# A language model tower on one core: mixer, dense layer and experts as one stage, with one written list of steps per engine

## What is computed

```python
h = layernorm(token_emb[ids] + type_emb[type] + pos_emb) * gamma + beta
h = h + attention(layernorm(h))                  # 8 heads of 192
x = layernorm(h)
z = layernorm(x) * g1 + b1                       # the mixer
q, k, v = split(z @ in_w.T + in_b)               # 12 heads of 16
x = x + (softmax(q @ k.T / 4) @ v) @ out_w.T + out_b
x = x + gelu(x @ mlp_w1 + mlp_b1) @ mlp_w2 + mlp_b2     # the dense layer, 192 -> 768 -> 192
xm = layernorm(x) * g2 + b2
gates = softmax over the 2 largest of xm @ gate_w.T + gate_b
for e in range(4):                               # the experts, each 192 -> 768 -> 192
    x = x + gates[e] * (gelu(xm @ w1[e] + b1[e]) @ w2[e] + b2[e])
return h + x
```

## Time and profile before

| | |
|---|---|
| three runs | 911.65 us median (911.03 to 914.28) |
| the profiled execution | 905.92 us, span from first to last instruction 904.2 us |
| PE, PEld busy | 804.1 us (89%), 721.8 us (80%) |
| DVE, ACT, POOL busy | 532.7 us (59%), 477.0 us (53%), 267.3 us (30%) |
| granted TensorE clock, mean | 0.963 |
| attention | 0 to 423.6 us |
| mixer | 423.6 to 587.4 us |
| dense layer | 594 to 654 us |
| experts | 654 to 904.2 us |

### The profile page before, as it was taken

The page is one execution under the profiler, slowest core; times in us unless marked ns, Lnnn a source line. Parts: engine busy times, 40 slices in busy tenths (PEclk is TensorE's granted clock), DMA queues, the critical chain, the costliest instruction groups (busy, mean ns, idle before and its releaser), DMA issues. The chain is left out here.

```text
span 904.2 us, 16184 instructions
## 1 busy us (share of the span) xinstructions
PE 804.1 (89%) x5880; PEld 721.8 (80%) x5880; DVE 532.7 (59%) x1404; ACT 477.0 (53%) x1282; POOL 267.3 (30%) x479
## 2 busy tenths in 40 slices
PE   0398999999999999986679897779899999999997
PEld 0298999999999999986558676668778898888987
DVE  4855454545555455345687777437877565665564
ACT  2255363635354444441575878555555665566654
POOL 6372020202020202021246779600207024061060
PEclk9999999999999999998786999899999999999999
DMA  8353333333332323331101111030000000000000
GB/s 241 99 107 71 78 73 71 80 70 80 71 80 70 80 70 79 72 80 45 48 1 62 63 62 41 23 93 1 1 1 1 1 18 1 19 1 1 18 1 18
DMA packets 33615, 47.30 MB, mean 52 GB/s; under 512 B 4672, under 2 KB 28608, under 8 KB 33536
## 3 DMA queue, kind: packets, MB, share of 16 engines
q1 hardware_dynamic: 28240, 34.63, 16.0%
q0 software_dynamic: 2544, 9.05, 3.4%
q10 hardware_dynamic: 2752, 2.59, 1.1%
HBM read 30.53 MB, written 15.73 MB: 51 GB/s over the span
## 5 line engine op out<-in xcount | busy, mean ns | idle before, releaser
L1524 DVE TENSOR_TENSOR ffn_hid_lo<-ffn_gelu,ffn_hid_hi 128x512 fp32r<-128x512 f32 x120 | 95.6, 799 | 105.4 <-ACT ffn_hid_hi L1498 104.2
L1452 PE MATMUL ffn_ps_out<-ffn_weights_w,ffn_hid_hi 128*128 128x384 f32 x480 | 144.1, 357 | 3.0 <-DVE ffn_hid_lo L1524 2.6
L1494 ACT ACTIVATE ffn_gelu<-ffn_ring,ffn_b 128x512 f32<-128x512 f32 x120 | 82.3, 686 | 110.8 <-PE ffn_ring L1441 107.1
L454 POOL TENSOR_SCALAR attn_probs<-attn_probs,attn_inverse 128x128 f32<-128x128 f32 x128 | 48.1, 376 | 288.4 <-DVE attn_inverse L744 280.6
L1453 PE MATMUL ffn_ps_out<-ffn_weights_w,ffn_hid_lo 128*128 128x192 f32 x480 | 120.6, 251 | 0.0
L1452 PEld LDWEIGHTS ffn_ps_out<-ffn_weights_w,ffn_hid_hi 128*128 128x128 f32 x480 | 90.0, 188 | 9.9 <-DVE ffn_hid_lo L1524 5.1
L1453 PEld LDWEIGHTS ffn_ps_out<-ffn_weights_w,ffn_hid_lo 128*128 128x128 f32 x480 | 91.3, 190 | 4.1
L937 POOL TENSOR_SCALAR mix_probs<-mix_probs,mix_inverse 128x128 f32<-128x128 f32 x192 | 73.9, 405 | 56.3 <-DVE mix_inverse L1188 56.3
L613 ACT ACTIVATE attn_probs<-ps_scores,attn_neg_max 128x128 f32<-128x128 f32 x128 | 45.4, 366 | 77.6 <-DVE attn_neg_max L740 77.6
L1498 ACT ACTIVATE ffn_hid_hi<-ffn_gelu 128x512 fp32r<-128x512 f32 x120 | 75.9, 632 | 3.8
L1382 POOL TENSOR_SCALAR ffn_bias_part<-ffn_b,ffn_gates 128x192 f32<-128x192 f32 x64 | 37.4, 602 | 134.9 <-DVE ffn_gates L1558 133.8
(11 more groups left out here) (272 smaller groups left out, 2182.8 us busy)
## 6 DMA issues: line engine op xcount, KB each, us to landing
v_rows<-attn_v_flat SPq DMA_DIRECT2D x16, 768.0 KB, 3.3
attn_v_rows<-v_rows SPq DMA_DIRECT2D x128, 96.0 KB, 3.7
mix_stage<-in_w POOLq DMA_DIRECT2D x5, 576.0 KB, 4.9
mix_stage<-in_w POOLq DMA_DIRECT2D x10, 192.0 KB, 3.3
mix_stage<-in_w POOLq DMA_DIRECT2D x5, 384.0 KB, 4.1
attn_stage_main<-in_w_qkv SPq DMA_DIRECT2D x2, 768.0 KB, 8.1
h_rows<-hin SPq DMA_DIRECT2D x8, 192.0 KB, 2.0
ffn_base<-h_rows SPq DMA_DIRECT2D x1, 1536.0 KB, 9.2
```

The lines of the kernel that those rows point to most:

```text
L454: last = nc.gpsimd.tensor_scalar(probs[:, n, j, :], probs[:, n, j, :], inverse[:, n, j:j + 1], float(D) ** -0.5, ALU.mult, ALU.mult)
L1452: nc.tensor.matmul(ps_out[:, b, 0:2 * D], hid_hi[:, i % 3, tile], w2[:, c, :, :], start=c == 0, stop=False)
L1494: nc.scalar.activation(gelu[:, i % 2, :], ring[:, bank("L1", i), :], ACT.Gelu, bias=b1[:, f * HC + c:f * HC + c + 1]).then_inc(chunk_read, 1)
L1524: nc.vector.tensor_tensor(hid_lo[:, i % 3, :], gelu[:, i % 2, :], raw(hid_hi[:, i % 3, :]), ALU.subtract).then_inc(lo_ready, 1)
```

## The change

`mixer` and `experts` become one function, `mixer_and_feed_forward`, one block. The numbers of what is computed stay the same.

- The dense layer is worked in 8 pairs of tiles as soon as a pair's mixer output is there. DX transposes its rows, D1 makes two hidden slices of 256 tokens in one bank (10 matmuls of 256 columns), DE is the gelu of each half on ACT, DG the hi copy, now on POOL, and the lo on DVE, D2 the second layer of one tile into a ring bank, DF the addition on DVE.
- Up to expert chunk 11 the order is no longer one list: `ORDERS` holds a list for each of PE, ACT, DVE and POOL. Behind that the old pattern goes on. Norms of the experts' rows (EN) of units 0 and 1 are in the lists, those of units 2 and 3 among the later chunks.
- Accumulators of the second expert layer are the banks of the mixer's scores, and buffers of the experts reuse memory of the mixer's; added waits guard both (`exps_ready`, `v_ready`, `out_filled`, `d2_filled`).
- Weight loads, expert constants and per-unit loads of h1 are issued from SP's queue, at the block's start for the first layer, instead of POOL's and ACT's. Weights 0 and 1 are split among the mixer's steps, 2 and 3 at the lists' end, 4 behind.

```diff
-def mixer(nc, keep, dram):
+def mixer_and_feed_forward(nc, keep, dram):
...
+    TWO = 2
+    PT = TWO * P
+    DENSES = TILES // TWO
+    BLOCKS = HC // 2
...
+        ORDERS = {
+            "pe": """X:0.0 X:0.1 Q:0.0 Q:0.1 Q:0.2 V:0.0 V:0.1 V:0.2 S:0 V:0.3 S:1 X:1.0 X:1.1 S:2 S:3 T:0 T:1 Q:1.0 S:4 A:0 Q:1.1 O:0 T:2 S:5 S:6 T:3 Q:1.2 A:1 T:4 S:7
...
+            "dve": """N:0.3 X:0.0 X:0.1 N:1.0 N:1.1 N:1.2 Q:0.1 Q:0.2 V:0.0 V:0.1 V:0.2 S:0 V:0.3 S:1 W:0.0 J:0 N:1.3 J:1 S:2 X:1.0 X:1.1 S:3 L:0 J:2 S:4 A:0 L:1 J:3 W:0.1
...
+        for i in range(FIRST, len(chunks)):
+            chunk(i)
...
+        def walk_order(engine, do):
+            for step, i in first_steps[engine]:
+                do[step](i)
+            for step, i in order:
+                if step in do:
+                    do[step](i)
...
+            def dense_his(i):
+                p, k = i
+                pool.wait_ge(d_gelu, BLOCKS * p + k + 1)
+                if p:
+                    pool.wait_ge(d2_filled, TWO * p)
...
+            def dense1(i):
...
+                slot_free("D1", i)
...
+                for c in range(2):
+                    cols, to = slice((2 * k + c) * P, (2 * k + c + 1) * P), slice(c * PT, (c + 1) * PT)
+                    for n, (w, x, part) in enumerate(passes):
+                        last = nc.tensor.matmul(ring[:, bank("D1", i), to], w[:, cols], x[:, part, :], start=n + c == 0, stop=n == 4 and c == 1)
...
+            def dense_gelu(i):
...
+                for c in range(2):
+                    part = slice(c * PT, (c + 1) * PT)
+                    last = nc.scalar.activation(dgelu[:, k, part], ring[:, bank("D1", i), part], ACT.Gelu, bias=b1[:, 2 * k + c:2 * k + c + 1])
```

More of the change, by code:

```diff
@@ L839, in mixer @@
[L839 to L877, removed]
@@ new lines, in mixer_and_feed_forward, with second, chunk @@
+        for part in range(3):
+            put(FIRST + part, ("H", (4, part)))
+            put(FIRST + part + 1, ("W", (4, part)))
+        def second(i):
+            order.append(("L2", i))
+            if i % HC == HC - 1:
+                order.append(("EF", i // HC))
+        def chunk(i):
+            early = i % HC == LAG - 1 and i >= LAG
+            if early:
+                second(i - LAG)
+            order.append(("L1", i))
+            if i >= LAG and not early:
+                second(i - LAG)
+            order.extend(after.get(i, ()))
@@ new lines, in steps_of @@
+        def steps_of(engine):
+            for word in ORDERS[engine].split():
+                kind, _, place = word.partition(":")
+                numbers = tuple(int(n) for n in place.split("."))
+                yield kind, numbers if len(numbers) > 1 else numbers[0]
+        first_steps = {engine: list(steps_of(engine)) for engine in ORDERS}
+        order = []
+        for i in range(FIRST, len(chunks)):
+            chunk(i)
+        for i in range(len(chunks) - LAG, len(chunks)):
+            second(i)
@@ L1045, in project_out, with turn_rows @@
                 last.then_inc(out_filled, 1)
-            walk_order({"X": transposes, "Q": project_qk, "V": project_v, "S": scores, "T": turn_probs, "A": mix, "O": project_out})
+            def turn_rows(to, t, main, tail):
+                nc.tensor.transpose(to[:, main], rows[:, t, 0:MAIN], keep["ident"][:, :])
+                for twin in (slice(0, TAIL), slice(TAIL, P)):
+                    last = nc.tensor.matmul(to[twin, tail], rows[:, t, MAIN:D], keep["ident"][:, :], start=True, stop=True)
+                return last
@@ new lines, in expert_rows @@
+            def expert_rows(i):
+                u, part = i
+                pe.wait_ge(xn_ready, u + 1)
+                slot_free("EX", i)
+                to = ring[:, bank("EX", i), :]
+                for b in range(UNIT):
+                    tile = slice(b * P, (b + 1) * P)
+                    if part == 0:
+                        last = nc.tensor.transpose(to[:, tile], xn[:, b, 0:MAIN], keep["ident"][:, :])
+                    else:
+                        for twin in (slice(0, TAIL), slice(TAIL, P)):
+                            last = nc.tensor.matmul(to[twin, tile], xn[:, b, MAIN:D], keep["ident"][:, :], start=True, stop=True)
+                last.then_inc(ex_filled, 1)
@@ L1645, in tower @@
             attention(nc, keep, dram)
[L1646 to L1650 removed]
+        mixer_and_feed_forward(nc, keep, dram)
 def host_layout(inputs):
```

757 lines of the change are left out of this document (394 added, 363 removed).

## The result

| | before | after |
|---|---|---|
| median | 912.96 us (911.03 to 915.14) | 886.03 us (884.57 to 892.9) |
| profiled execution, its span | 905.92, 904.2 us | 884.57, 882.8 us |
| start of the stage | 423.6 | 422.6 |
| first dense matmul | 593.8 | 484.3 |
| expert chunk 12 (the mark) | 692.1 | 669.5 |

A forecast was written before the change was run, and what follows sets the result against it. PE bounds the dense layer and experts, but no engine fills the mixer. 423.6 + 242 + 215.7 = 881.3 us against a 904.2 span, 22.9 less; taken off the median 911.65, this gives 889 us, range 869 to 910.

The forecast's parts named there:

- The start: Mixer stage's beginning up to the first dense matmul: 60 us, between 54 and 67, holding 32.6 us of PE work.
- N:0.3 and its wait for the constants: DVE's hin normalisation for unit 0, ahead of the first lo split, delays Q, K and first scores by 5 to 7 us.
- lower bound of 54: Shortest time allowed from stage start to first dense matmul, in us: holes filled and the wait for constants absorbed.
- The pace behind the start: First dense matmul to expert chunk 12: 164 us of PE work at 0.90 of full-clock pace, 182 us.
- Engines' sums: Work from stage start to expert chunk 12: PE 196.6 us and fullest, DVE 173.6, ACT 173.
- After the mark: From expert chunk 12 to the end: 212.1 us plus 3.6 for two sets of norms, 215.7.
- norm set: Norms of one unit's expert rows; those of units 2 and 3 now fall behind chunk 12, charged 1.8 us each.
- The sum: Whole kernel: 423.6 + 242 + 215.7 = 881.3 us against a span of 904.2, 22.9 less.
- Rival B: Mixer queues run nearly as densely as the experts: start 54, pace 0.95, total 873 us; chance 0.16.
- Rival C: ACT's table switches set the pace: 14 loads on PE's path add 18 us, total 907; chance 0.15.
- Rival D: Mixer holes stay unused, PE still waiting for POOL's probabilities before each transpose half: 923 us, slower; chance 0.13.

The follow-up runs named there:

- e2_weights_later: Changed kernel with POOL's hi copies of the second weight set moved behind the normalisation of half 6; 878.79 us, ratio 0.9647.
- e3_both: Changed kernel with POOL's second-weight hi copies behind half 6's normalisation and DVE's unit 0 hin scaling behind the first reciprocal; 874.82 us, ratio 0.9597.
- after_again: The changed kernel run once more, unaltered, as neighbour for the other runs; 889.98 us, ratio 0.9763.
- e6_no_switch: Changed kernel with Exp in place of the dense layer's Gelu, so 12 tables are loaded instead of 22; 887.93 us, ratio 0.9751.

## Why the prediction was right

- **The start.** Forecast 60 us to the first dense matmul, measured 61.7. The two halves of it were not both right. N:0.3 and its wait for the constants were named with the time of the lo split, 433 against 433.0 measured; the run without it puts its price at 5.5 us. The holes behind it do fill better than of old: between 440 and 460 us PE is busy 17.1 us, where it was 11.8. But the step "SP, whose queue waits there for nothing that anyone needs sooner" is false. What SP loads at 464.6, POOL needs ahead of Z:5, and this costs 11.2 us. So 60 came out by luck. In e2_weights_later, which has the forecast wait and not the other, the first dense matmul stands 54.0 us behind the first transpose of the stage (477.8 and 423.8): the forecast took the filling of the holes for 6 us too little, and the wait that it denied gave them back. In e3_both, with both waits gone, it is 50.7 us (474.8 and 424.1), below the lower bound of 54.
- **The pace behind the start.** Forecast 0.90 of full clock for 164 us of PE work, measured 164 / 185.2 = 0.885. In after_again it is 0.87 and in e3_both 0.875. So the number holds, but its two parts are off. The 0.80 that served as the lower bound is PE's busy share in the mixer; its full-clock pace was 106.2 / 163.8 = 0.65. And PE's work was put too low: between the first dense matmul and the mark PE is busy 173.6 us at a mean clock of 0.99, where 164 had been added up, and idle for only 11.6 us. The holes fill better than the forecast had it (busy 0.94 of the stretch), and the steps take some 8 us longer than their prices. Which steps do was not looked into. The clock was right in this profile (over 0.93 forecast, 0.97 to 1.00 seen); in after_again it is 0.95 from the first dense matmul to the mark.
- **Engines' sums.** DVE was put at 174 us up to the mark, ACT at 173. Between 422.6 and 669.5 they have 177.1 and 168.7, and PE has 212.8 (196.6 forecast at full clock), so the order of the engines stands.
- **After the mark.** 215.7 forecast, 213.3 measured. The price of a norm set was the term mis-sized: 1.8 us each forecast, 1.2 for both together (213.3 - 212.1), and 0.6 to 1.1 in the other traces. The old difference of 62.6 and 59.0 us between units was mostly the stage's start: the two new units from logits to logits that hold the norm sets (from 694.48 to 753.97 and to 814.06) take 59.5 and 60.1.
- **The sum.** Span 22.9 us less forecast, 21.4 measured. The start is 1.7 over, the stretch to the mark 3.2 over, the stage's begin 1.0 and the part after the mark 2.4 under, which leaves 1.5. The medians differ by 26.9 in this comparison and by 20.4 in the next, 889.98 and 886.03 against the forecast 889.
- **Rival B** (start 54, pace 0.95, 873 us) falls for this kernel with the pace of 0.885. e3_both comes out at 874.82 by another way: its start is 50.7 us and its pace 0.875.
- **Rival C** falls with e6_no_switch: 18 us had been set for ACT's loads on PE's path, and without ten of them the time is the same. The Trainium skill (ScalarE: Activation LUTs, "What ACT_TABLE_LOAD costs") adds a drain of 1.38 us to each switch. The trace agrees on the 1.28 us of the load but shows 1.31 from the end of the gelus (509.57) to the first exponential (510.88), so here the measurement decides against the drain. "Table sets: the hidden batching unit" of the same page advises against what the change does; where ACT has 168.7 us of work up to the mark and PE 212.8, it costs nothing that was measured.
- **Rival D** (holes not used) falls with the pace. Its mechanism, PE standing before POOL's probabilities, is what happened once, for 7.3 us, and there because POOL stood behind a DMA.

What stays open: in after_again the stage starts at 423.9 and reaches the mark after 254.5 us, 7.6 more than in the first profile of the same kernel. Its clock is 0.68 up to 460 us and 0.75 from there to 484, where the first has 0.73 and 0.79, and 0.89 and 0.94 in the next two windows instead of 0.97 and 1.00. The waits are alike in length (10.5 and 6.1 against 10.7 and 7.3). PE works there without a hole from 477.3 to 495, at a clock of 0.50 from 480 to 485, 0.57 to 490 and 1.00 from there; in the first profile it is at 1.00 from 480 on, 4 to 5 us behind its own hole. Why the clock came back later was not tried.

## What to carry to other kernels

When orders are written out, go through each list for steps that depend on a DMA and ask what stands behind them: a split of weights that are first multiplied at 618 us stood one place ahead of a step of the critical loop at 465 and cost 11 us by the medians, while ten table loads cost nothing that could be told from the spread. A single staging buffer ties that DMA to the last reader of the previous load, on another engine. A fill order is worth what its neighbours leave open: the same dense steps in the same form took 120 us behind the mixer, and the kernel was 70 us slower that way than with them among the mixer's steps. So a piece must be judged in the mixture, and a wait of 2 us in one list should be moved only after a look at what its producer itself waits for.

## What was unexpected of the hardware

A hole in PE can cost more than its length, and not the same in every execution. The waits of PE for POOL taken away with H:1.0 to H:1.2 were 6.2 us, and the median fell by 11.2 us: by 6 against the executions with a mean clock of 0.976, by up to 14 against the one with 0.962. In the same place the matmul of 192 columns took 0.41 us behind the hole and 0.27 us later. The reverse was seen too: 8.5 us less waiting at the very start, where the clock is low in any case (0.68 before 460 us with the wait, 0.77 without), brought 5.5 us. There 1.9 us came back as longer waits for POOL (8.0 to 9.9), and the window of 460 to 484.3 had clock 0.65 instead of 0.75:

```profile
460.00:484.30 24.30, 16.38 (x109) 13.58 (x106) 12.25 (x38) 11.16 (x42) 9.19 (x21) 0.65 0.18 58
```
